# A graph, attention and slice-attention block: centring 50 tiles on GpSimd instead of VectorE

## The reference, cut to what matters

```python
xn = layernorm(x)
x = x + gnn(xn, src, dst) + mix(xn)      # two message layers; a mixing block
x = x + slice_attention(layernorm(x))

# in mix: h = logmap0(xn) (a factor a row times xn), then
h = conv1d(h, w_qkv)                     # one row a sample: only the middle tap counts
mean, var = mean(h), var(h)              # over all 6250 nodes, for each of 768 channels
h = relu(gamma * (h - mean) / sqrt(var + 1e-5) + beta)
# in gnn: agg = segment_sum(xn[dst], src), a gather of 100,000 rows of 256 and a sum by node
```

## Time and profile before

| | |
|---|---|
| median of 3 runs | 3236.68 us (3227.99 to 3247.08) |
| profiled execution: span from first to last instruction | 2941.0 us |
| median less span (no time of the profiled execution itself is listed) | 295.7 us |
| busy in the span: PE, ACT, POOL, DVE | 2160.4, 1623.8, 1645.0, 1404.0 us |
| 83.5 to 200 us: DVE, PE, ACT, POOL busy | 105.9, 77.8, 29.1, 0.0 us |
| 298.4 to 1420 us: DVE, PE, ACT, POOL busy | 462.6, 846.9, 684.2, 757.9 us |
| mean granted TensorE clock | 0.862 of 2.4 GHz |

### The profile page before, as it was taken

The page is one execution under the profiler, slowest core; times in us unless marked ns, Lnnn a source line. Parts: engine busy times, 40 slices in busy tenths (PEclk is TensorE's granted clock), DMA queues, the critical chain, the costliest instruction groups (busy, mean ns, idle before and its releaser), DMA issues.

```text
span 2941.0 us, 33881 instructions
## 1 busy us (share of the span) xinstructions
PE 2160.4 (73%) x8805; PEld 1594.9 (54%) x8805; DVE 1404.0 (48%) x3188; ACT 1623.8 (55%) x3910; POOL 1645.0 (56%) x1745
## 2 busy tenths in 40 slices
PE   0652677777778887669477778778777657999989
PEld 0441456565556665545355666556665545555577
DVE  8899513443434443318423434344343216999511
ACT  7410465666566666536556666666666533655322
POOL 0000777777777777740477777777777771344200
PEclk9875688998888898888788989888898877899979
DMA  7200333333333333352333333333333348200002
GB/s 181 70 18 0 99 108 109 113 111 111 113 113 111 113 110 108 110 142 66 105 108 110 114 113 110 111 114 113 110 110 109 108 115 187 58 18 9 1 18 70
DMA packets 101270, 280.79 MB, mean 95 GB/s; under 512 B 29211, under 2 KB 43369, under 8 KB 97088
## 3 DMA queue, kind: packets, MB, share of 16 engines
q0 software_dynamic: 75904, 210.74, 25.0%
q1 hardware_dynamic: 12184, 55.08, 7.1%
q10 hardware_dynamic: 13000, 12.80, 1.5%
HBM read 252.91 MB, written 25.60 MB: 95 GB/s over the span
## 4 chain that ended last, share of the span: by engine, by line
POOL 49%; issue 18%; PE 16%; DVE 15%; ACT 1%; DMA 1%; DVEq 0%; SPq 0%; ACTq 0%; PEldq 0%; POOLq 0%
POOL big L566 49%; DVE arena_a L1277 3%; PE ps L1243 3%; DVE arena_a L1278 3%; PE ps L1149 3%; PE ps L1116 2%; PE ps L1138 2%; PE ps L1030 1%; DVE big L1714 1%; PE ps L1235 1%; PE ps L1132 1%; DVE big L1715 1%; DVE arena_b L1695 1%; PE ps L1147 1%; DVE lnst L1321 1%
## 5 line engine op out<-in xcount | busy, mean ns | idle before, releaser
L566 POOL DMA_INDIRECT big<-table,arena_a x1568 | 1509.3, 963 | 703.8 <-issue 476.8
L1030 PE MATMUL ps<-big 128*125 x3968 | 1080.2, 433 | 505.5 <-SPq L461 272.5
L1030 PEld LDWEIGHTS ps<-big 128*125 128x125 f32 x3968 | 840.4, 216 | 714.5 <-issue 560.0
L1610 DVE TENSOR_TENSOR big<-ps,big 125x257 f32 x496 | 211.1, 426 | 1260.4 <-PE ps L1030 1240.0
L697 ACT ACTIVATE arena_b<-iota_row,arena_a 128x125 f32<-128x125 f32 x1984 | 601.3, 386 | 60.6 <-PE ps L1030 25.5
L699 ACT ACTIVATE big<-arena_b,ones 128x1000 f32<-128x1000 f32 x248 | 280.1, 1129 | 8.1
L720 ACT ACTIVATE nodes<-nodes 125x512 f32<-125x512 f32 x50 | 31.6, 632 | 305.0 <-DVE nodes L1668 304.8
L1664 DVE RECIPROCAL nodes<-nodes 125x512 f32<-125x512 f32 x50 | 167.7, 3354 | 1.7
L1049 PE MATMUL ps<-arena_b,nodes 128*125 128x384 f32 x400 | 162.2, 530 | 0.0
L594 POOL TENSOR_TENSOR arena_b<-arena_b,head 125x512 f32<-125x512 f32 x50 | 55.0, 1100 | 159.1 <-DVE head L1722 159.1
L555 POOL IOTA big<- 1x992 f32 x1 | 0.9, 948 | 195.3 <-DVEq L1400 195.3
(11 more groups left out here) (385 smaller groups left out, 3029.0 us busy)
## 6 DMA issues: line engine op xcount, KB each, us to landing
big<-table,arena_a POOLq DMA_INDIRECT x1568
table<-nodes SPq DMA_DIRECT2D x9, 1120.0 KB
nodes<-table SPq DMA_DIRECT2D x4, 1680.0 KB
nodes<-table ACTq DMA_DIRECT2D x50, 125.0 KB
mix_rows<-nodes ACTq DMA_DIRECT2D x50, 125.0 KB
nodes<-in_x_dram SPq DMA_DIRECT2D x5, 1120.0 KB
big<-mix_rows SPq DMA_DIRECT2D x5, 1120.0 KB
nodes<-in_x_dram SPq DMA_DIRECT2D x10, 560.0 KB
```

Source lines behind the costliest of these rows:

```text
L566: pool.indirect_dma_start(gat[:, GRP * slot + k, 0:D], None, table[l], bass.IndirectOffsetOnAxis(ap=s_dst[:, n:n + 1], axis=0)).then_inc(s ...
L1030: mm = pe.matmul(ps[0:PT, SUM_BANKS[q % SB], 0:257], onehot[:, ROUND * (r % 2) + QS * k + n, :], gat[:, bass.ds(slots[QS * k + n], 1), :]. ...
L1610: dve.tensor_tensor(at, ps[0:PT, SUM_BANKS[q % SB], 0:257].unsqueeze(1), at, ALU.add).then_inc(s("agg_added"), 1)
```

## The change

Centring leaves VectorE's turns. GpSimd does it in one run of 50 tiles, between its constants and its wait for `prods_ready`, and with two instructions a tile: a TENSOR_SCALAR (nodes times the row's factor) into the ring, a wait for its own semaphore, and a TENSOR_TENSOR that subtracts the mean row in place. The waits for `xn_ready`, `mu_ready` and `centred_used` go with it. Apart from that, the two wait tables `need_row` and `free_row` hold 16 bit numbers and not 32 bit ones, which moves the tables behind them in their buffer.

```diff
-        need_row, o = carve(arena_a, o, [2, NQ], I32, 1)
+        need_row, o = carve(arena_a, o, [2, NQ], U16, 1)
...
-        free_row, o = carve(arena_a, o, [2, NGRP], I32, 1)
+        free_row, o = carve(arena_a, o, [2, NGRP], U16, 1)
...
             pool.sem_inc(s("consts_set"), 1)
+            pool.wait_ge(s("mu_ready"), 1)
+            for t in range(NT):
+                pool.wait_ge(s("xn_ready"), t + 1)
+                if t >= HIN:
+                    pool.wait_ge(s("centred_used"), t - HIN + 1)
+                po.link(pool.tensor_scalar(hin[:, t % HIN, 0:D], nodes[:, t, :], fac[:, t:t + 1], None, ALU.mult))
+                pool.tensor_tensor(hin[:, t % HIN, 0:D], hin[:, t % HIN, 0:D], mu[0:PT, :], ALU.subtract).then_inc(s("centred"), 1)
             pool.wait_ge(s("prods_ready"), 1)
...
-            def centre_tiles(level, back):
-                for t in range(*GRAM_TILES[level, back]):
-                    if t == 0:
-                        dve.wait_ge(s("mu_ready"), 1)
-                    dve.wait_ge(s("xn_ready"), t + 1)
-                    if t >= HIN:
-                        dve.wait_ge(s("centred_used"), t - HIN + 1)
-                    dve.scalar_tensor_tensor(out=hin[:, t % HIN, 0:D], in0=nodes[:, t, :], scalar=fac[:, t:t + 1],
-                                             in1=mu[0:PT, :], op0=ALU.mult, op1=ALU.subtract).then_inc(s("centred"), 1)
-
...
             def in_gap(level, back):
 
-                if level <= 13:
-                    centre_tiles(level, back)
                 if (level, back) == (14, 0):
```

## The result

The changed kernel took 3250.03 us (median of 20 runs, 3240.08 to 3262.96) against 3238.39 of the kernel before in 20 runs beside it: a ratio of 1.0033, 95% interval 1.002 to 1.0046. It is slower by about 11 us. 23 had been forecast: the sign was right, the size was about twice what came. By the mark of 16 us that the prediction set for a change that can be told from none, this counts as no change, to which it had given 0.28.

The account below looks back on a forecast made before the run. GpSimd's gathers were taken as the bound from 298 us to layer 0's end, delayed one for one by VectorE's sort. 2941.0 - 4.2 + 27 = 2964 us of span; on the median 3236.7 + 23 = 3260 us, range 3238 to 3281.

Parts of the forecast that it names:

- Rival B: In the sort, GpSimd and VectorE don't disturb each other, so the 4.2 us of the turns are won: 3232.5 us; chance 0.11.
- 295.7 us "around the span": Time outside the profiled execution's span of 2941.0 us, taken to stay unchanged up to the median of 3236.7 us.
- 33 x 0.83 = 27 us: In the sort, 33 tiles meet VectorE's exchanges and each holds VectorE up by 0.83 us: 27 us added.
- Rival C: GpSimd falls behind in centring, so TensorE waits for tiles and VectorE for TensorE: 3281 us; chance 0.12.
- Who comes second waits for the whole of the other's instruction: GpSimd and VectorE take turns when both read SBUF; read from last-stage pairs, applied to the sort's exchanges.
- lower end of 18 us: Smallest price of contention in the sort: 33 tiles at 0.54 us, 0.39 for the TENSOR_TENSOR and 0.15 for the TENSOR_SCALAR.
- Rival D: Contention exists, but most tiles are centred in turns and first exchanges, 14 remaining at 0.83 us: 3245 us; chance 0.09.
- I take 0.40: Duration in us assumed for GpSimd's TENSOR_SCALAR on a tile, bounded by 0.25 and 0.63 from the nearest rows.
- The gain in the turns: 4.2 us: Removing VectorE's centring shortens the six turns of half 1 by 0.70 us each, those of half 0 by nothing.
- 2.8 us more of cover: At the sort's end, the chain behind TensorE's last tile is done at 188.1 us, while VectorE comes only at 190.94.
- First gather near 321: Sign to look for in the changed profile: GpSimd's first gather starts near 321 us instead of 298.4.
- The tables, 0 give or take 1: 16 bit wait tables could move the gathers' 0.9 us of ring waits by 1 us either way, taken as 0.

Follow-up runs that it names:

- t3: Changed kernel with no centring on any engine, GpSimd only passing the waits and counting: 3234.71 us, ratio 0.9979 to the kernel before.
- t4: ScalarE scales each tile in one instruction, mean subtraction left out, GpSimd and VectorE not taking part: 3234.0 us, ratio 0.9978 to the kernel before.
- t7: Changed kernel with two GpSimd memsets of the tile in place of its two instructions: 2939.51 us, against 2947.0 for the kernel before on that chip.
- t6: Changed kernel with GpSimd's TENSOR_TENSOR alone for each tile, the factor left out: 2957.16 us, against 2947.0 for the kernel before on that chip.
- t2: The changed kernel unaltered, timed once more beside the kernel before: 3246.18 us, ratio 1.0024.
- t1: Kernel before with only the two wait tables made 16 bit, centring staying on VectorE: 3237.61 us, ratio 0.9994.
- t5: Changed kernel with GpSimd's TENSOR_SCALAR alone for each tile, no mean subtracted: 2943.1 us, against 2947.0 for the kernel before on that chip.

## Why the prediction was right in sign and wrong in size

- **The mechanism was right.** GpSimd and VectorE hold each other up when both read SBUF (t3, t4 and t7 take away the reading and the loss goes), exchanges with a PSUM operand are left alone, and the sort's delay goes to the end undiminished. Rival B is out by 11.0 us. That the gathers are bound by GpSimd was read from an execution on a chip of another kind; 295.7 us "around the span" should have been a warning, since no other row accounted for them.
- **The term that was mis-sized: "33 x 0.83 = 27 us".** It measured 12.6 (11.0 in the exchanges, 1.6 in the flips). Both factors were too large. The count: 28 of VectorE's instructions (23 in the exchanges and 5 of the 6 flips) met the TENSOR_TENSOR and 26 the TENSOR_SCALAR, not 33 each, because a GpSimd that gets one tile through in two exchanges can't bring more than 51 / 2 of them into 51 exchanges; a slower helper collides less often. Rival C had this count, 27 tiles for the exchanges, but the sum went by 33. The price: 0.32 or 0.41 for the first (two of 0.53), not 0.53 throughout; 0.08 or 0.16 for the second, not 0.30. "Who comes second waits for the whole of the other's instruction" had been taken from pairs in the last stage, and it is no rule for the sort: here a TENSOR_SCALAR of 1.74 us costs its partner 0.08. The lower end of 18 us failed by both as well: 12.6 us are 0.46 for each of some 27 tiles, against 0.54 for 33. Rival D's 3245 us lies nearer to the 3250.03 than the forecast does, but by luck: it had 14 tiles within the exchanges, not 27.
- **TENSOR_SCALAR: "I take 0.40", between 0.25 and 0.63.** It takes 0.92 alone, outside of both bounds. The upper bound had rested on the thought that an instruction with one input can't take longer than one with two. For the time of the kernel it mattered at the end (below), and because it spaces the meetings with the TENSOR_TENSOR (t6).
- **Half of the rule cited stands.** Of "SBUF — State Buffer", "Who interferes with whom" in the Trainium skill, the trace agrees that reading SBUF on both sides is what collides (t7). That one engine blocks the other for its whole length it doesn't bear out for a TENSOR_SCALAR: 0.08 to 0.16 us of 0.92. For the TENSOR_TENSOR it comes near: in the rows above L560 ends 94.92 - 94.34 = 0.58 us after the L1285 it met, and the L1284 behind it ends 95.40 - 94.92 = 0.48 us after L560, so most of each runs after the other.
- **The gain in the turns: 4.2 us.** It is 3.1 in this execution, 4.1 in that of the same kernel in t2, and 4.0 without any centring (t3). The difference is the last turn: it takes 2.27 us here, where the others take 1.50 to 1.78, and 1.50 in t2. TensorE's transposes there took 1.76 us here, and 0.99 in t2 and in the kernel before. The rows around these transposes, of the kernel before, of the changed one and of t2:

```profile
178.50:181.40 2.90, 0.99 (x9) 0.92 (x9) 2.64 (x7) 0.22 (x1) 0.00 (x0) 1.00 0.00 0
```

```profile
188.90:190.90 2.00, 1.92 (x8) 1.89 (x9) 0.00 (x0) 0.51 (x2) 1.92 (x3) 0.50 0.02 4
```

```profile
189.00:190.00 1.00, 0.94 (x8) 0.94 (x9) 0.00 (x0) 0.24 (x1) 1.00 (x2) 1.00 0.00 0
```

(length, busy PE, PEld, DVE, ACT, POOL, granted clock.) The granted clock is 1.00, the 2.4 GHz level, in the first and the third and 0.50, the 1.2 GHz level, in the second. The second and the third are the same kernel, so this microsecond belongs to the execution and not to the change. Why the clock fell in one of them is open.

- **"2.8 us more of cover" at the end.** It was counted for a GpSimd that keeps up at 1.13 us a tile. Within the exchanges it makes one in 2.87 us, TensorE waited for it 14 times and 14.4 us in all, and when the exchanges end the chain behind the last tile is still ahead: +3.25 us. Some 2.1 us of it are TensorE's clock. The granted clock is 0.50 from 198.5 to 204.3 us and was 1.00 from 181.3 to 188.2 before; the last tile's four matmuls (L918) take 2.08 us and the two groups of the chain 0.59 and 2.07 (L931), where at 1.00 a tile took 1.13 and the chain 0.38 and 1.13. t2 has the same three long durations. The prediction took the chain at its old length. This is the part of rival C that came true, at a third of the 11 us it put on late tiles.
- **"First gather near 321."** It was 311.2. With the terms measured, 298.4 + 12.6 - 3.1 + 3.25 = 311.2.
- **The tables, 0 give or take 1:** t1 shows no cost.
- **What a gather waits for:** the prediction's list left out the 131.5 us for a DMA between the layers, which stand in the earlier trace rows. Nothing of its sum rests on this.

## What to carry to other kernels

Before an elementwise instruction is moved to an idle engine, look at what that engine shares with the busy one: GpSimd's reads of SBUF cost VectorE's two-SBUF-input instructions 11 us here, while the same tiles scaled on ScalarE cost them nothing, and that version is faster than both kernels. The price of such a collision goes by meetings, by kind, and not by busy time: a measured duration of each kind of pair is worth more than a rule. And a span far from the time that it is compared with calls for a second look: in every run here with both on record, 1.8 to 1.9 us lie around the span, so a gap of 295.7 meant another execution.

## What had not been expected of the chip

- GpSimd's TENSOR_SCALAR of 125x256 f32 took 0.92 us with factors from SBUF and 0.84 with a constant; its TENSOR_TENSOR of the same size, with twice the input, 0.63.
- A meeting costs GpSimd more than VectorE: TENSOR_SCALAR goes from 0.92 to 1.74 us, the exchange beside it from 0.62 to 0.70.
- Flips, with 896 columns of one SBUF input, went from 0.69 to 0.94 and 1.03 beside the TENSOR_TENSOR in the changed kernel and t2. They stayed at 0.69 in t5, t6 and t8, but there no instruction of GpSimd ran beside them, so these runs say nothing on flips.
- The same one-core kernel takes 2947 us on one chip and 3237 to 3269 in the other groups, with a granted TensorE clock of 0.862 and 0.859 (before, t5) against 0.81, and GpSimd waiting 0.9 to 2.2 us for the ring against 315 to 360. Which of the two leads to the other is open.
